# Five prefetched weight halves issued with the last batch's loads instead of in two later groups

## The reference

```python
x = x + xattn(layernorm(x), ctx, ctx, ctx)      # (8,100,512), ctx (8,722,512)
#   x1 = x @ ctx^T ; h = gelu_tanh(x1) * x1 ; h @ ctx
x = x + ffn(layernorm(x))
#   logits = x @ router_w ; e = argmax(logits) ; w = sigmoid(logits[e])
#   out = (gelu(x @ w1[e] + b1[e]) @ w2[e] + b2[e]) * w
#   w1: (16,512,1024)  w2: (16,1024,512), all float32
```

## Time and profile before

| | |
|---|---|
| median of 3 runs | 310.06 us (309.59 to 310.96) |
| profiled execution, its own time | 313.14 us |
| its span, first to last instruction | 311.4 us |
| mean granted TensorE clock | 0.917 |
| TensorE matmuls busy | 246.1 us (79%) |
| VectorE, POOL, ScalarE busy | 120.0, 98.8, 32.1 us |
| moved by DMA | 100.41 MB, mean 322 GB/s |
| weight halves | 64 of 1 MB, median 18.6 us from issue to landing |

### The profile page before, as it was taken

The page is one execution under the profiler, slowest core; times in us unless marked ns, Lnnn a source line. Parts: engine busy times, 40 slices in busy tenths (PEclk is TensorE's granted clock), DMA queues, the critical chain, the costliest instruction groups (busy, mean ns, idle before and its releaser), DMA issues.

```text
span 311.4 us, 10067 instructions
## 1 busy us (share of the span) xinstructions
PE 246.1 (79%) x3668; PEld 172.9 (56%) x3669; DVE 120.0 (39%) x405; ACT 32.1 (10%) x75; POOL 98.8 (32%) x141
## 2 busy tenths in 40 slices
PE   0899999999999884397778877987984678859850
PEld 0858768768678351154456665655663456536540
DVE  3034536446444466133334333444433134324320
ACT  0411111021021120010010101010110011000100
POOL 2002314224123155003523334435343133241353
PEclk9999999999999955597999979999999599977995
DMA  7999799999999994089699968999999999999910
GB/s 258 370 372 355 271 343 360 372 309 408 336 394 380 400 376 160 26 290 385 200 352 378 372 221 302 355 367 364 378 362 388 361 422 362 390 361 388 354 36 21
DMA packets 20698, 100.41 MB, mean 322 GB/s; under 512 B 5232, under 2 KB 6224, under 8 KB 11464
## 3 DMA queue, kind: packets, MB, share of 16 engines
q1 hardware_dynamic: 15044, 93.02, 81.2%
q0 software_dynamic: 4928, 6.60, 6.7%
q10 hardware_dynamic: 708, 0.55, 0.6%
HBM read 95.58 MB, written 4.97 MB: 323 GB/s over the span
## 4 chain that ended last, share of the span: by engine, by line
PE 47%; DMA 24%; issue 10%; SPq 9%; DVE 2%; POOL 2%; POOLq 2%; ACTq 2%; DVEq 1%; ACT 0%
PE bank L308 14%; PE bank L315 14%; DMA W<-in_w 10%; DMA area<-rows 10%; PE bank L396 8%; SPq L228 8%; PE bank L385 5%; PE bank L323 2%; DMA id_out<-tok_at 2%; DMA rows<-nothing,pad_at 1%; ACTq L209 1%; PE bank L404 1%; PE bank L293 1%; PE bank L299 1%; DMA xs<-in_x 1%
## 5 line engine op out<-in xcount | busy, mean ns | idle before, releaser
L385 PE MATMUL bank<-W,area 128*32 128x256 f32 x992 | 66.5, 405 | 23.2 <-DMA W<-in_w 12.0
L396 PE MATMUL bank<-W,area 128*32 128x128 f32 x1984 | 65.8, 287 | 3.9 <-issue 3.0
L396 PEld LDWEIGHTS bank<-W,area 128*32 128x32 f32 x1984 | 56.0, 115 | 9.2 <-issue 4.2
L795 POOL DMA_INDIRECT out<-area,at_out x32 | 32.7, 1022 | 85.5 <-DVE area L672 49.4
L385 PEld LDWEIGHTS bank<-W,area 128*32 128x32 f32 x992 | 34.1, 115 | 45.4 <-issue 25.6
L315 PE MATMUL bank<-area,hidT 128*100 128x512 f32 (+1 forms) x96 | 46.8, 601 | 0.0
L308 PEld LDWEIGHTS bank<-xnT,area 128*128 128x128 f32 (+1 forms) x384 | 44.3, 193 | 4.3 <-issue 4.3
L308 PE MATMUL bank<-xnT,area 128*128 128x100 f32 (+1 forms) x384 | 44.6, 278 | 1.0 <-issue 1.0
L491 ACT ACTIVATE area<-area 128x256 f32<-128x256 f32 x31 | 12.9, 416 | 172.5 <-PE bank L396 150.7
L209 POOL DMA_DIRECT2D area<-rows x32 | 24.5, 765 | 18.3 <-issue 18.2
L672 DVE SCALAR_TENSOR_TENSOR area<-bank,area 128x128 f32 x31 | 10.9, 351 | 42.7 <-PE bank L396 24.5
(11 more groups left out here) (86 smaller groups left out, 156.4 us busy)
## 6 DMA issues: line engine op xcount, KB each, us to landing
W<-in_w SPq DMA_DIRECT2D x64, 1024.0 KB, 18.6
area<-in_ctx_main SPq DMA_DIRECT2D x8, 1280.0 KB
area<-in_ctxT_a SPq DMA_DIRECT2D x8, 768.0 KB, 10.0
area<-in_ctxT_b SPq DMA_DIRECT2D x8, 676.0 KB, 9.2
area<-rows POOLq DMA_DIRECT2D x32, 65.5 KB, 7.2
xs<-in_x SPq DMA_DIRECT2D x8, 200.0 KB
area<-in_ctx_rest SPq DMA_DIRECT2D x8, 160.0 KB
out<-area,at_out POOLq DMA_INDIRECT x32
```

Source lines behind the costliest of these rows:

```text
L385: last = nc.tensor.matmul(p_h[U * q:U * q + U, 0:FQ], curT[:, U * k:U * k + U], mine, start=(k == 0), stop=(k == KD - 1), tile_position=(0 ...
L396: last = nc.tensor.matmul(p_y[U * q:U * q + U, 0:DQ], hT[:, U * c:U * c + U], W2[:, slot, c, DQ * q:DQ * q + DQ], start=(c == 0), stop=(c ...
L795: nc.gpsimd.indirect_dma_start(out_q, bass.IndirectOffsetOnAxis(ap=at_out[r][:, :], axis=0), y_out[:, r, :], None, bounds_check=last_out, ...
```

## The change

The count for the last batch goes from 2 to 7, and the two groups of held loads with their waits are gone. The same 16 halves are issued in the same order.

```diff
@@ -44,7 +44,7 @@
-EARLY = (0, 0, 1, 1, 1, 2, 4, 2)
+EARLY = (0, 0, 1, 1, 1, 2, 4, 7)
@@ -266,10 +266,6 @@
                     sp.dma_start(b2q.rearrange("q (e d) -> q e d", e=E),
                                  b2.rearrange("e (q d) -> q e d", q=Q)).then_inc(s_b2, 16)
-            sp.wait_ge(s_att, NB)
-            load_weights(2)
-            sp.wait_ge(s_land, AHEAD)
-            load_weights(4 * SLOTS - sum(EARLY) - 2)
 
 
             sp.wait_ge(s_plan, 1)
```

## The result

The changed kernel takes 314.05 us (median of 4 runs, 313.60 to 315.95) beside 310.51 us for the kernel before: ratio 1.0121, 95% interval 1.0074 to 1.0169. Measured twice more beside other kernels it gave 1.0058 (1.0030 to 1.0086) and 1.0106 (1.0051 to 1.0160), 1.0095 in the mean, some 3 us. It is slower, where the forecast was 310.0 us and no change, and 314.05 lies above the range's end of 313.2. The profiled execution took 315.95 us with a span of 314.3 (before: 313.14 and 311.4).

What follows compares the result with a forecast made beforehand. The weight stream at the end was taken to hang on TensorE freeing slots; 3.8 - 1.2 - 2.7 = -0.1 us at 149 us was carried to the end, giving 310.0 us from 310.06, range 307 to 313.2.

Steps and rivals of the forecast that it cites:

- What bounds the kernel: Whole kernel: the end hangs on a weight stream restarting at 187 us, its start on when TensorE frees a slot.
- the rival of the stream: Whole kernel bound by bytes: the three halves come off its end, 8.2 us, giving 301.8 us; chance 6%.
- the two halves for the last attention: Halves held for `s_att`: issuing them early changes nothing, since they land near 118.1 us as now.
- Term 1, the pads: Start of stage two: three weight halves ahead make the last pad land at 128.5 us, +3.8; bounds 0 to +6.1.
- three halves landed by 127 us: Sign to check after 118 us: the three weight halves moved ahead are all in by 127 us.
- turns between queues: Alternative for the pads: a pad waits for one half's share of weights, landing at 127.4 us, +2.75 instead of +3.8.
- Term 2, `id_out`: Load of output places before POOL's loop: on empty engines it takes 4.4 instead of 5.61 us, -1.2 us.
- Term 3, the first turns of POOL's loop: Transposes for units 3 and 4: gap 3.95 instead of 6.67 us, -2.7 us; bounded at -1.0 if the clock falls.
- Unit 5's rows: Row load issued at 146.3 us meets two weight halves; the transpose at 154.85 could be 0 to 0.8 us late, 0 taken.
- third rival (small transfers starve): Pads and unit 0's rows stay behind the three halves: stage two starts 6.1 us late, 314.0 or 312.3 us; chance 27%.

Runs made afterwards that it cites:

- delayed start: Kernel before, with 18 tiny activations on ScalarE between its wait for the pads and the loads of units 1 to 3: ratio 1.0122 (1.0074 to 1.0169).
- two early: Kernel before, with the hold for the last attention dropped and two of the other three held halves issued early, one still held: ratio 1.0046 (1.0012 to 1.0079).
- one early: Kernel before, hold for the last attention dropped, one of the other three held halves issued early: ratio 0.9947, repeated 0.9980.
- one early with the output places between: Kernel before, last-attention hold dropped, one of three other halves early, `id_out` load moved between the loads of units 1 and 2: ratio 1.0003 (0.9967 to 1.0040).

## Why the prediction was wrong

**What bounds the kernel** was read rightly: the dry queue twice behind the three halves, the stream's start hanging on TensorE's slots, everything behind shifted with it. The delayed start is the cleanest test of it, and the rival of the stream (301.8 us) failed. That the two halves for the last attention cost nothing held too.

**Term 1, the pads: the step that failed first.** The prediction put +3.8 us "by the bytes"; it was 129.16 - 124.68 = +4.5. What was mis-sized is the end of the transfers. It let weights and pads run through at 378 GB/s until 127.7 and added 0.8 us. In fact the engines had less to move (2.13 MB of weights, 1.25 of the pads' queue and 0.07 of row loads after 118 us, 9.1 us at that rate, so until 127.1), but they worked at half their share from 124 to 129 us, and the last half and the last pad both came in at 129.2 to 129.3. So this tail cost 2.1 us and not 0.8. The prediction's own sign, three halves landed by 127 us, failed with it. With two or three halves early every pad took 6.7 to 8.7 us; with none, 2.9 to 4.5, where no other transfer of the chain ran beside it. A better number stood in the rows: the scatters' median of 8.4 gives 120.69 + 8.4 = 129.1. I took their longest as a bound (+5.3) and went by the bytes. The rule of the Trainium skill that was weighed there, turns between queues ("DMA: Bandwidth & Descriptors", Queues, rings and completion order), gave +2.75 when one turn was taken to be a whole half's share. The trace agrees that the queues move side by side (0.31 MB of q1 and 0.09 MB of q0 from 118 to 119 us). The last pad's 8.47 us lies between one such turn (6.6) and two (9.4), and no run here shows how many were taken.

**Term 2, `id_out`**: -1.2 put, 5.61 - 5.03 = -0.6 measured. The middle between the bounds was too hopeful; where no weights ran beside it, it took 4.9 to 5.1 us in each of five executions.

**Term 3, the first turns of POOL's loop**: -2.7 put, 4.46 - 6.67 = -2.2 measured. The gap closed and the clock held, as forecast. The pace of 3.95 us, from 154.85 to 158.80, was too short for this place: unit 3's first layer started 0.41 us after TensorE was free, waiting for no one, and made it 4.46.

Sum: 4.5 - 0.6 - 2.2 = +1.7 us at the transpose for unit 4, against -0.1. **Unit 5's rows**: the prediction took 0 and kept 0.8; they took 8.19 us, and the cost was 0.3. So +2.0 us arrive at 157 us, and the last weight half is issued 1.7 us late. All four misses go the same way. Three are transfers: between a row in full engines and one in empty ones I chose toward the middle, and they kept near the slow end. The fourth is the pace of term 3.

**The rest** up to the 3 us of the runs is not settled. Of the span's 2.9 us, 0.8 is the longer stretch at the lower clock near 283 us; a late start alone of 3.4 us gave a ratio of 1.2%, which is 3.8 us, so the carried part may be a little over one to one, but the interval holds one to one as well. The forecast missed a change by a sum of small misses of one sign (0.7, 0.6, 0.5 and 0.3 us), none of them outside the bounds of its term. The forecast gave slower by more than 0.5% a chance of 27% and named the mechanism as its third rival (small transfers starve), with the point from which it decides at 5.5 us. That point was wrong with terms 2 and 3: with their measured sizes it is 1.6 + 0.6 + 2.2 = 4.4 us, and the pads were 4.5 late.

## What to carry to other kernels

A bulk transfer that is moved into a hole is not free if small transfers of the critical chain are issued there: price each of them at its whole latency in full engines, read from a row of the same trace, and not by the bytes in front of it. Ask first whether the bulk is waited for at all; if its queue runs dry later anyway, earlier bytes buy nothing. How much may go early is found by what has landed when the last small transfer goes out, here one half of three. That share cost nothing; a gain it did not show.

## What the hardware showed that I had not expected

A transfer of 128 rows of 2 KB took more than twice as long beside about 1 MB of weights as without them. With 0.01 MB of weights or less still to move after 121 us, the last pad took 2.90, 3.24, 3.55 and 3.86 us (one early twice, one early with the output places between, before); with 1.06, 1.23, 1.43 and 1.48 MB it took 8.72, 8.47, 7.73 and 8.15 (two early, and the three executions of the changed kernel). Within the second group the time does not rise with the bytes. Whether it rises in a step or a slope between the groups is not shown: the one execution there (0.49 MB, 6.67 us) had the load of `id_out` beside it, and that load alone went with a pad of 6.08 us.

TensorE stood at one fixed place in unit 4's first layer, after 30 of 32 matmuls, in all sixteen profiled executions, waiting for no one. The stall goes with the engines' share in the 3 us before it: 3.16, 3.25, 1.64 and 1.26 us where that share was 0.99 to 1.05; 0.81 to 0.99 where it was 0.86 to 0.92; 0.18 to 0.76 where it was 0.50 to 0.77. So something that TensorE needs there seems to come through the same engines. Code that is loaded behind weights would fit, but the packets of the queue of kind "instruction" do not show it: before the two longest stalls the last such packet was at 148 us and at 141 us, and none fell into the stall. The cause stays open.
